# Routing weights spread by DMA, weights split once, routing in halves, and other attention rings: an eight-layer kernel on one core

## The reference

```python
scores = jax.nn.sigmoid(x @ gate_weight.T)                  # 32 routed experts, top 2 of 4 groups, top 6
cw = (jax.nn.one_hot(topidx, E, dtype=x.dtype) * tw[..., None]).sum(1)      # weight of each token and expert
eo = jnp.einsum('tei,eih->teh', jax.nn.silu(g) * u, w_down)                 # g, u: x by w_gate, w_up; 64 wide
routed = jnp.einsum('te,teh->th', cw, eo)
shared = jax.nn.silu(x @ shared_w_gate) * (x @ shared_w_up) @ shared_w_down
anchor = jnp.einsum('tl,tlh->th', acw, ao)                                  # 16 anchors, 32 wide, one per token
out = routed + shared + ANCHOR_ALPHA * anchor
```

## Time and profile before

| | us |
|---|---|
| median of 3 runs (1840.86 to 1844.87) | 1843.44 |
| the profiled execution, its own time | 1840.44 |
| its span, first to last instruction | 1838.7 |
| la | 0 to 361 |
| lb, ld | 361 to 543, 606.5 to 788 |
| lc, le, lg | 543 to 606.5, 788 to 1125.6, 1379 to 1579.4 |
| lf, lh | 1125.6 to 1379 (253.4), 1579.4 to 1838.7 (259.3, with the store of x) |

### The profile page before, as it was taken

How to read it: one execution, slowest core, us unless ns; L and a number is a source line. 1 busy time by engine, 2 the same in 40 slices (tenths; PEclk the granted TensorE clock), 3 DMA queues, 4 the chain that set the end, 5 groups by cost and what they waited for, 6 DMA issues and landing times. The chain is left out here.

```text
span 1838.7 us, 26374 instructions
## 1 busy us (share of the span) xinstructions
PE 1435.4 (78%) x9138; PEld 950.7 (52%) x9138; DVE 1223.6 (67%) x2818; ACT 730.5 (40%) x1218; POOL 759.3 (41%) x944
## 2 busy tenths in 40 slices
PE   3899999728976259974898895699994685569997
PEld 2323222227864248832665664577762484447775
DVE  6766666363565745576998997766658636776665
ACT  2376666521113212156543441444444211244443
POOL 3821211027611166302565664455552230545555
PEclk9699999958999569987999997799997697579999
DMA  2210100000110001000000002100000000210000
GB/s 74 68 52 19 58 2 1 24 1 24 34 22 1 24 12 35 23 17 1 1 1 1 1 1 60 30 1 1 1 1 6 1 1 1 60 30 1 1 1 23
DMA packets 39332, 32.70 MB, mean 18 GB/s; under 512 B 13856, under 2 KB 33392, under 8 KB 39216
## 3 DMA queue, kind: packets, MB, share of 16 engines
q1 hardware_dynamic: 39216, 31.21, 6.2%
HBM read 29.99 MB, written 1.21 MB: 17 GB/s over the span
## 5 line engine op out<-in xcount | busy, mean ns | idle before, releaser
L429 DVE CUSTOM_DVE_ANT_1 la_neg<-bank,la_table 128x512 f32<-128x512 f32 x256 | 165.8, 688 | 63.2 <-PE bank L520 63.2
L1690 DVE SCALAR_TENSOR_TENSOR xn<-xn,bank 128x512 f32<-128x512 f32 x144 | 99.0, 687 | 140.1 <-PE bank L1705 138.6
L1340 PEld LDWEIGHTS bank<-le_diag,le_dtxT 128*128 128x128 f32 x1024 | 126.5, 191 | 80.5 <-issue 59.0
L1340 PE MATMUL bank<-le_diag,le_dtxT 128*128 128x128 f32 x1024 | 142.0, 282 | 25.4 <-DVE le_h L1258 21.2
L1258 DVE TENSOR_TENSOR_SCAN le_h<-le_keep,bank 128x512 f32<-128x512 f32 x128 | 155.2, 1213 | 3.8 <-PE bank L1340 3.8
L1589 ACT ACTIVATE xn<-bank 128x512 f32<-128x512 f32 x144 | 86.1, 598 | 167.4 <-PE bank L1705 166.9
L356 ACT ACTIVATE la_probT<-bank 128x512 f32<-128x512 f32 x256 | 139.1, 598 | 25.9 <-PE bank L539 23.9
L1548 POOL TENSOR_TENSOR lf_h_low<-lf_wu,lf_h_high 128x512 fp32r<-128x512 f32 x84 | 109.3, 1301 | 90.5 <-ACT lf_h_high L1574 90.5
L1548 POOL TENSOR_TENSOR lh_h_low<-lh_wu,lh_h_high 128x512 fp32r<-128x512 f32 x84 | 109.3, 1301 | 90.3 <-ACT lh_h_high L1574 90.3
L1196 ACT ACTIVATE le_keep<-le_dt,le_A 128x512 f32<-128x512 f32 x128 | 92.2, 722 | 133.0 <-DVE le_h L1258 133.0
L1111 POOL TENSOR_TENSOR le_hc<-le_hc 128x512 f32<-128x512 f32 x64 | 81.0, 1266 | 101.4 <-DVE le_hc L1267 97.6
(11 more groups left out here) (599 smaller groups left out, 3698.9 us busy)
## 6 DMA issues: line engine op xcount, KB each, us to landing
la_table<-la_scratch SPq DMA_DIRECT2D x4, 1792.0 KB, 6.6
la_bias_parts<-la_scratch_parts SPq DMA_DIRECT2D x12, 248.0 KB, 5.8
lb_w1s<-in_L_ffn_w_dram SPq DMA_DIRECT2D x8, 256.0 KB, 2.7
lb_w2s<-in_L_ffn_w_dram SPq DMA_DIRECT2D x8, 256.0 KB, 3.1
ld_w1s<-in_L_ffn_w_dram SPq DMA_DIRECT2D x8, 256.0 KB, 2.7
ld_w2s<-in_L_ffn_w_dram SPq DMA_DIRECT2D x8, 256.0 KB, 3.1
out_dram<-x SPq DMA_DIRECT2D x1, 1024.0 KB, 5.1
le_win<-in_L_attn_a_w_in_dram SPq DMA_DIRECT2D x1, 256.0 KB, 2.7
```

The costliest lines, as they stand in the source:

```text
L429: dve.tensor_tensor_reduce(out=neg[:, u % 2, :].rearrange("p (c i) -> p c i", i=P), in0=k.bank[u % RING1][:].rearrange("p (c i) -> p c i", ...
L1340: last = pe.matmul(k.bank[4 + q % 2][:, j * P:(j + 1) * P], dtxT[:, (g * G2 + bb) * TPB + j, c, :], diag[:, d % DIAGS, j, :], start=True, ...
L1690: dve.scalar_tensor_tensor(gated[:, n % 2, :], sl, 1.0 if t < ET else ALPHA, up, ALU.mult, ALU.mult).then_inc(gated_ready, 1)
```

## The change

Token layers: `spread`, its matmul and the three bf16 parts are gone. The weights (32 routed and 16 anchor rows, float32) are turned, stored to `lf_scratch` in DRAM, and for each unit but the shared tile's SP loads a 128 x 512 tile of `lf_weight` (256 KB), in which each of 2 (or 4) rows of the scratch is repeated on 64 (or 32) partitions: 80 loads a layer, ring of 4 (WR). DVE multiplies silu by the weight first, and by up second; silu stays in its PSUM bank. Banks for gate and up grow from two pairs to three (GB), `hidden` and its parts from 3 to 4 (RING), the lag of down from 2 to 3. Early tiles stand between the others (ORDER: six late, one early, three times). The routing is made for 1024 tokens ahead of the loop, and for the other 1024 in pieces between units of the first chunks. The split weights come from DRAM: la writes them there once, in nine pieces of 896 columns that POOL splits in its later steps. Products without use (`idle_products`) stand in the heads.

Attention: RING1, RING2 go from 3, 3 to 2, 4. Experts: of the first expert's 16 picks POOL makes 8 and DVE 8; POOL's loop is written out; idle products stand at the start, near the end of the slot search and before the first gather.

The core of the diff:

```diff
+    def idle_products(self, pe, count, bank):
+
+        for _ in range(count):
+            pe.matmul(self.bank[bank][:], self.ident16[:], bcast(self.ident16[:, 0:1], (0, 4), (1, P)), start=True, stop=True)
...
-    RING1, RING2, NPT, NSLOT = 3, 3, 8, 3
+    RING1, RING2, NPT, NSLOT = 2, 4, 8, 3
...
+                if g == 1:
+                    load_piece(0)
+                    load_piece(1)
+                if g >= 2:
+                    for i in (range(0, 4) if g == 2 else range(4, PIECES)):
+                        store_piece(i)
+                        if i + 2 < PIECES:
+                            load_piece(i + 2)
...
+                pool.tensor_copy(high, raw).then_inc(piece_high, 1)
+                pool.wait_ge(piece_high, i + 1)
+                pool.tensor_tensor(low, raw, high.bitcast(F32), ALU.subtract).then_inc(piece_split, 1)
+                if 5 <= n < 5 + PIECES:
+                    pool.wait_ge(v1_ready, n - 1)
+                    split_piece(n - 5)
...
+            for e in range(E):
+                s = e % 2
+                if e >= 2:
+                    pool.wait_ge(pick_used, e - 1)
+                pool.tensor_copy(own[:, s, :], slots[:, e, :]).then_inc(own_ready, 1)
+                pool.wait_ge(own_ready, e + 1)
+                for n in range(SHARED if e == 0 else B):
+                    for j in range(n * TPB, (n + 1) * TPB):
+                        last = pool.tensor_scalar(pick[:, s, j, :], number[:], own[:, s, j:j + 1], None, ALU.is_equal)
+                    last.then_inc(pick_ready, 1)
...
+            for n in range(SHARED, B):
+                for j in range(n * TPB, (n + 1) * TPB):
+                    last = dve.tensor_scalar(pick[:, 0, j, :], number[:], slots[:, 0, j:j + 1], None, ALU.is_equal)
+                last.then_inc(pick_by_dve, 1)
...
+            k.idle_products(pe, 16, 7)
...
+            pe.wait_ge(slots_near, 1)
+            k.idle_products(pe, 22, 1)
...
+            k.idle_products(pe, 12, 1)
...
-    STK = 3 * E + L
-    RING, LAG = 3, 2
+    STK = E + L
+    GB, RING, LAG, WR = 3, 4, 3, 4
+    ORDER = [t for i in range(EARLY) for t in (*range(i * LATE // EARLY, (i + 1) * LATE // EARLY), LATE + i)]
+    NO_WEIGHT = ORDER.index(TILES - 1)
...
+        scratch = nc.dram_tensor(f"{tag}_scratch", [STK, B * T], F32)
+        weight = sb("weight", [P, WR, T])
...
+        SECOND_TURNS = {TILES + 9: 2, TILES + 12: 3}
+        SECOND_DUE = TILES + 8
...
+            def store(c):
+                at = slice(c * T, (c + 1) * T)
+                sp.wait_ge(stackT_ready, c + 1)
+                sp.dma_start(scratch[:, at], stackT[:, at]).then_inc(stackT_stored, 16)
+
+            store(0)
+            store(1)
+            for u in range(U):
+                c, s, t = place_of(u)
+                if u == 2 * TILES - WR:
+                    store(2)
+                    store(3)
+                if s == NO_WEIGHT:
+                    continue
+                n = weighed_before(u)
+                if u == 0:
+                    sp.wait_ge(stackT_stored, 32)
+                if u == 2 * TILES:
+                    sp.wait_ge(stackT_stored, 64)
+                if n >= WR:
+                    sp.wait_ge(gated_ready, n - WR + 1)
+                first, rows = (t * P // I, P // I) if t < ET else (E + (t - ET) * P // AI, P // AI)
+                row = bass.AP(scratch, first * B * T + c * T, [[B * T, rows], [0, P // rows], [1, T]])
+                sp.dma_start(weight[:, n % WR, :], row).then_inc(loaded_weight[n % WR], 16)
 
...
-            link(pool.memset(spread[:], 0.0))
-            for part in range(3):
-                v = spread[:, 0:ET * P].rearrange("r (e i) -> r e i", i=I)
-                link(pool.affine_select(out=v, in_=v, compare_op=ALU.not_equal, fill=1.0, base=-E * part,
-                                        pattern=[[-1, E], [0, I]], channel_multiplier=1))
...
-                    last = pool.tensor_copy(high[:, piece], raw[:, piece])
-                last.then_inc(high_ready, 1)
-                pool.wait_ge(high_ready, n + 1)
-                for raw, high, low in ((wu, wu_high, wu_low), (wg, wg_high, wg_low)):
-                    last = pool.tensor_tensor(low[:, piece], raw[:, piece], high[:, piece].bitcast(F32), ALU.subtract)
...
+            for _ in route(0):
+                pass
+            second = route(1)
...
-                    v = late(u)
-                    sl, up = silu[:, v % 2, :], k.bank[2 + v % 2][:, :]
+                    v = late_before(u)
+                    sl, up = k.bank[v % GB][:], k.bank[GB + v % GB][:]
                     dve.wait_ge(silu_ready, v + 1)
-                    dve.wait_ge(up_done, v + 1)
                 else:
                     sl, up = silu_e[:, t - LATE, c * T:(c + 1) * T], up_e[:, t - LATE, c * T:(c + 1) * T]
+                if s != NO_WEIGHT:
+                    n = weighed_before(u)
+                    dve.wait_ge(loaded_weight[n % WR], 16 * (n // WR + 1))
+                    dve.scalar_tensor_tensor(gated[:, n % 2, :], sl, 1.0 if t < ET else ALPHA, weight[:, n % WR, :], ALU.mult, ALU.mult)\
+                       .then_inc(gated_ready, 1)
+                    dve.wait_ge(gated_ready, n + 1)
+                    sl = gated[:, n % 2, :]
                 if u >= RING:
                     dve.wait_ge(h_low_ready, u - RING + 1)
-                if t == TILES - 1:
-                    dve.tensor_tensor(hidden[:, u % RING, :], sl, up, ALU.mult).then_inc(hidden_ready, 1)
-                else:
-                    n = spreads(u)
-                    dve.scalar_tensor_tensor(gated[:, n % 2, :], sl, 1.0 if t < ET else ALPHA, up, ALU.mult, ALU.mult).then_inc(gated_ready, 1)
-                    dve.wait_ge(gated_ready, n + 1)
-                    dve.wait_ge(spread_done, n + 1)
-                    dve.tensor_tensor(hidden[:, u % RING, :], gated[:, n % 2, :], k.bank[4 + n % 2][:, :], ALU.mult).then_inc(hidden_ready, 1)
-                if c and t == LAG + 1:
+                if t < LATE:
+                    dve.wait_ge(up_done, v + 1)
+                dve.tensor_tensor(hidden[:, u % RING, :], sl, up, ALU.mult).then_inc(hidden_ready, 1)
+                if u < SECOND_DUE:
+                    next(second, None)
+                if u == SECOND_DUE:
+                    for _ in second:
+                        pass
+                if c and s == LAG + 2:
                     add_acc(c - 1)
             add_acc(B - 1)
 
...
-                if t < TILES - 1:
-                    n = spreads(u)
-                    if n >= 2:
-                        pe.wait_ge(hidden_ready, tile_of_spread(n - 2) + 1)
-                    pe.matmul(k.bank[4 + n % 2][:], spread[0:STK, t * P:(t + 1) * P], stackT[:, c * T:(c + 1) * T], start=True, stop=True)\
-                        .then_inc(spread_done, 1)
```

More of the change, by code:

```diff
@@ L238, in group_at, with loads_before @@
             return n if r == 0 and 0 <= n < GROUPS else None
+        weights = k.token_weights
+        PIECES = weights.PIECES
+        def loads_before(i):
+            return sum(len(weights.pieces[j]) for j in range(i % 2, i, 2))
         block = ctx.enter_context(nc.Block())
@@ L243, in _, with load_piece, store_piece @@
         def _(sp):
+            def load_piece(i):
+                if i >= 2:
+                    sp.wait_ge(piece_split, i - 1)
+                for place, source in weights.pieces[i]:
+                    sp.dma_start(place(split_raw[:, i % 2, :]), source).then_inc(piece_loaded[i % 2], 16)
+            def store_piece(i):
+                which, at = weights.place(i)
+                sp.wait_ge(piece_split, i + 1)
+                sp.dma_start(weights.high[which][:, at], split_high[:, i % 2, :].bitcast(F32)).then_inc(piece_stored[i % 2], 16)
+                sp.dma_start(weights.low[which][:, at], split_low[:, i % 2, :].bitcast(F32)).then_inc(piece_stored[i % 2], 16)
             sp.dma_start(w1c[:], w1_rpe.rearrange("a h -> h a"), allow_slow_non_contiguous=True).then_inc(loaded_r, 16)
@@ L840, in _ @@
             pe.wait_ge(part_made, 3)
-            for n in range(B):
-                gather(0, 0, n)
+            for n in (0, 2, 1, 3):
+                gather(0, 0, n, True)
+            pe.wait_ge(pick_by_dve, B - SHARED)
             with pe.Fori(0, E // 2 - 1) as i:
@@ L1430, in layer_moe_tokens @@
         score = sb("score", [P, NT, E])
-        sc, cw, rest = (k.xnT[:, i * T:(i + 1) * T].rearrange("p (j e) -> p j e", e=E) for i in range(3))
-        masked, low, work, work1 = (k.xn[:, i * TPB:(i + 1) * TPB, :].rearrange("p a (b e) -> p (a b) e", e=E) for i in range(4))
-        hi = sb("hi", [P, NT * NG, GE // 2])
-        lo = sb("lo", [P, NT * NG, GE // 2])
-        hi2 = sb("hi2", [P, NT * NG, GE // 4])
-        lo2 = sb("lo2", [P, NT * NG, GE // 4])
-        t2 = sb("t2", [P, NT * NG, GE // 4])
@@ L1452, in layer_moe_tokens @@
-        silu = k.xn[:, 0:2 * TPB, :].rearrange("p (s j) d -> p s (j d)", s=2)
```

(16 more changed lines are left out.)

436 lines of the change are left out of this document (249 added, 187 removed).

## The result

The changed kernel takes 2188.79 us (median of 4 runs, 2183.87 to 2194.34) against 1842.72 us: ratio 1.188, interval 1.186 to 1.189. The profiled execution took 2189.06 us, its span is 2187.3 us. The forecast was 2216 us.

What follows compares the result with a forecast made beforehand. PE's ten matmuls a unit (2.30 us) bound the kernel before; weight loads on few engines would bound it after. +406 (lf, lh) - 17 (la) - 16 (lb, ld) = +373 on 1840.4: 2213, as median 2216 us; range 1715 to 2400.

Steps and rivals of the forecast that it cites:

- The mechanism: Token loops lf and lh: weight loads get 2 or 4 DMA engines, 5.60 us a routed load, +203 us a layer.
- the smaller of the two sides decides: Weight loads: DRAM side's 2 or 4 outermost, not the 128 partitions, sets the engines: 2 for 64 loads, 4 for 16.
- They add up: Token loops: all loads share the lowest engines, so their times sum: 100.8 us a chunk, 403 us for four.
- However deep the ring: Token loops: the loads' times sum to 403 us a layer whatever number of weight tiles the ring holds.
- the signs that the prediction named: Loop of lf: period 5.6 us, DVE waiting for lf_weight, landing some 20 us, DMA share 0.12 at 47 GB/s, clock 0.5.
- a landing in 2.7 us needs all 16 engines: Earlier 256 KB loads with 128 partitions on both sides: 2.7 us to landing taken to need 16 engines at 23.4 GB/s.
- The tail: End of lf after the last load, through DVE, ACT, POOL, PE and the last turning: some 7 us.
- The rings: Attention la: four banks for biased scores, two for plain ones, put at -21 us of la's net -17.
- the two sizes behind the 21: la: 25.6 us gained (0.20 us wait in each of 128 steps), 5 us lost by plain scores with two banks.
- a warm PE: lb and ld: PE at warm clock for the first expert's gather and products, 1.5 us of -8 a layer.
- The rival that all 16 engines carry the loads: Token loops: loads land in about 3 us and hide, layer -33 us, kernel 1744 us (1705 to 1790); chance 0.30.
- 27.5 less 9 in the sum: Rival with 16 engines, token loop: -27.5 us over four chunks, +9 for 23 units at DVE's pace with routing pieces.

Runs made afterwards that it cites:

- run 4: Changed kernel with each routing row stored two or four times in DRAM, routed loads [4][32] or [8][16]: 1836.27 us with two copies, 1759.54 us with four.
- runs 2 and 3: Changed kernel; 2: loads read different split-weight rows, outermost still 2 or 4, 2195.21 us; 3: one row for all 128 partitions, 128 outermost, 1747.13 us.
- run 7: Changed kernel with every second weight load issued by ACT on its own queue, shapes unchanged: 2188.79 us.
- run 6: Changed kernel with a ring of six weight tiles in place of four (WR = 6): 2191.57 us.
- run 5: Changed kernel with one load per row, repeats outermost (64 or 32), 192 issues a layer in place of 80: 1745.96 us, 0.949 of before.
- run 9: The kernel with one load per row (run 5) without the idle products: 1747.7 us.
- run 10: The kernel with one load per row (run 5) with all 16 first picks on POOL, none on DVE: 1763.88 us.

## Why the prediction was right

**The mechanism was the forecast's.** A load whose DRAM side has 2 or 4 outermost runs on 2 or 4 engines: shown by the count of tiny packets, by the period that halves with twice the engines (run 4), and by runs 2 and 3, which part the shape from the repetition. That the smaller of the two sides decides was my choice from the earlier trace rows, which show only loads that are equal on both sides; the runs bear it out, and with it the Trainium skill's rule ("DMA: Bandwidth & Descriptors", section "Why a DMA increments its semaphore by 16 and not by 1"), which names both access patterns. "They add up" is shown by the 49 GB/s of the loop, and that they share the same engines whatever the queue by run 7; that these are the lowest ones no run shows. "However deep the ring" came true in run 6, though there SP's issue kept the ring from filling. Of the signs that the prediction named, the period (5.35 us for 5.6), the wait of DVE, the DMA share (0.13 at 49 GB/s for 0.12 at 47) and a clock of 0.50 in stretches (1266 to 1274 us) are there; a landing time of these loads, put at some 20 us, is in no view of the changed kernel.

One reading in it does not hold: that a landing in 2.7 us needs all 16 engines. At its own 23.4 GB/s an engine, 16 of them carry 262144 B in 0.7 us, and 2.7 us is the rate of four; the time to landing does not tell the number of engines. The sum of the forecast does not use it.

**The sizes, for lf.** The first load was to be issued at +44.3 us: it is at +45.6 (1142.3 against the start of lf at 1096.7). The routed load was put at 5.60 us, from 23.4 GB/s an engine in a short window; it is 5.35, 24.5 GB/s an engine. From the first issue to the last multiplication with a weight (1531.3) that makes 389 us in place of 405. The tail took 8.1 us, not 7. Two times 16 us of faster loads, less 8 us of later heads, longer tails and a smaller gain in la, are the 24 us between 2213 and 2189.

**la** gained 14.2 us where I had 17. The rings gave 18 (I had 21), and 4 came back, as put, though this part varies. That the second biased product waited for an exponential was right, but the two sizes behind the 21 were both too small, and that these errors nearly cancel is luck. The 0.20 us of one step does not stand in all 128: half of the pairs have no wait at all, and the earlier trace rows sum the idle time to 6.9 us, not 25.6. Measured by starts, biased products and the step into them gained 29 us and the plain ones lost 13 (I had 25.6 and 5), with some 1.5 us less elsewhere.

**lb and ld** gained 16.5 us together, I had 16, and the parts agree too. From the first gather to the next the first expert is 6.1 us shorter in lb and 6.3 in ld, where I had 4.6 for the picks and 1.5 for a warm PE; the first gather comes 2.5 and 1.4 us earlier, where I had 2 for the logits. But the idle products are not shown to be the reason: run 9, without them, loses little, and the start of the last logits product of lb, 15.6 us into the layer in the changed kernel and 17.9 before, is 17.9 in run 5, which has them, and 15.6 in run 9. In the first expert the full clock goes with the shared picks, which spare PE most of its waits (run 10); run 9, which has the picks but no idle products, takes 10.0 us from the first gather of lb to the next, run 5 takes 9.3 and run 10 16.1.

**The rival** that all 16 engines carry the loads was put at 1744 us; with the loads made that way (run 5) it is 1746. The saving of the token layers is 33 us each, as its sum said, and its parts hold as well: in lf the first product down comes 15.2 us earlier (52.6 us into the layer, 67.8 before; put at 15), and from there to the end of the layer it is 17.6 us less (27.5 less 9 in the sum). So the idea of the change holds, and one line of it, a load with 2 or 4 rows outermost, cost 443 us.

## What to carry to other kernels

Look at the outermost dimension of both sides of every transfer that is issued in a loop: where one of them is 2 or 4, the transfer ran on 2 or 4 engines here, at some 24.5 GB/s each, and neither a larger ring nor a second queue helped. A broadcast of a few rows to many partitions is better written as one load per row, with the repeats outermost, than as one load with the rows outermost. And a transfer's duration is not to be taken from another of the same size: its packets, above all the tiny ones that close it, tell how many engines it had.

## What was not expected of the hardware

The store of eight copies from one tile to DRAM ran at 127 GB/s, with 32 tiny packets for two stores and thus on 16 engines each, where loads of before moved 232 and 278 GB/s.

SP's issue instruction can itself be slow. In the changed kernel it takes 3.8 us at the median, with a ring of six (run 6) 5.2 us, with 192 issues on 16 engines (run 5) 0.45 us. Few engines alone do not make it slow: with two queues sharing the loads it is 0.48 us on SP and 0.49 on ACT, at the same rate of the loop (run 7), and with two copies, where DVE waits for the loads as well, 0.52 us (run 4). In the changed kernel the first four issues of lf take 0.6, 0.5, 2.6 and 5.0 us, as if one queue took two loads on 2 engines at once and held the next; no run tests that. The tile's view of the changed kernel, min/median/max ns of the first entry:

```profile
L1639 SPq DMA_DIRECT2D lf_weight<-lf_scratch x80: 505/3778/6541, 1142.3 to 1516.7; - x80
```
